# The LoRA part of a bias, summed on VectorE instead of by TensorE products

## Chip, cores and metric

The kernel runs on one core of a Trainium2 chip. The metric is device time in microseconds (us) for one execution. Before the change three runs took 56.14, 56.83 and 57.04 us, a median of 56.83 us.

## What is computed

There are 8 samples `b` of 512 tokens and 256 channels, and a condition vector of 8 gates `g` for each sample. Two residual layers follow each other:

```python
# layer 0: 8 expert matrices mixed by the gates, under a mask
w_bot = einsum('bg,got->bot', cond, weight * mask)
x = x + einsum('bnt,bot->bno', x, w_bot) + bias0
# layer 1: a base matrix and 8 gated LoRA experts of rank 16, SCALING = 2
out = einsum('btc,oc->bto', x, W_base) + b_base
h = einsum('btc,erc->bter', x, As)
x = x + out + SCALING * einsum('bter,eor,be->bto', h, Bs, cond)
```

All data are float32. The kernel merges both layers into one matrix M(b) = W1(b) W0(b) for each sample and applies it to the transposed tokens. What is left beside the matrices is one bias per sample and output channel: bias0 + b_base + W_base bias0 + SCALING * sum over (e, r) of cond[b, e] B[e, o, r] (A[e, r] . bias0). The last summand is the LoRA part of the bias. In it, 8 experts times rank 16 give 128 pairs (e, r), the number of partitions.

## The kernel before

The program is written by hand for five engines with explicit semaphores; each engine runs its list in order. P is 128 partitions, NT = 2 halves of the 256 channels, NB = 8 samples.

**Stages.** TensorE first runs 28 warm-up products and the LoRA products that make W1 of samples 0 to 3 (`lora_first`, `lora`). Then come 32 products in `mixed` (line 532), float32 with a 128-column moving side, that mix the layer-0 experts; VectorE multiplies each result by the mask into W0 (`w0`). Every matrix that enters a merge or an apply is split into a high and a low float32r part, and a `product` adds three terms: high times high (line 463), high times the second low part (line 467) and the first low part times high (line 471). From sample 2 on, TensorE's list is merge(b+1), apply(b) in turn, with `lora_pair(6)` behind apply(2).

**Who prepares what.** For a sample b in the loop:
- GpSimd (POOL) adds the identity to W0 (`eye(b)`, line 203), and makes W0_lo (`w0_lo(b)`, line 199) and W1_lo (`w1_lo(b)`, line 193). `merge(b)` waits for W1_lo(b) before its first product (line 545).
- ScalarE (ACT) makes W1_hi (`w1_hi`, 242), W0_hi (248), M_hi from PSUM (`m_hi`, 255), x_hi (262), and stores half 0 of the output with its bias (`out0`, 271). `out0(0)` waits for `bias_done` (267); behind it in ACT's list are w0_hi(4), split_x_hi(3), w1_hi(4), m_hi(3) and out0(1).
- VectorE (DVE) makes x_lo (`split_x_lo`, 360), M_lo from PSUM (`m_lo`, 367), half 1 of the output (`out1`, 375), and W1 of two samples at once from PSUM (`w1_pair`, 340). In its list behind the bias come out1(0), split_x_lo(2), m_lo(2), w1_pair(4), out1(1), split_x_lo(3), m_lo(3), out1(2), split_x_lo(4). `w1_hi(4)` waits for both halves of w1_pair(4), and `w1_lo(4)` waits for w1_hi(4).

**The bias.** ACT copies a row of bias0, which every partition holds, into PSUM (`ps_row`, line 295). VectorE takes the dot products of A's rows with it (`dot(A_er, A_bias0)`, 423; one number for each pair (e, r), on that pair's partition), scales it by the gates to `low_bias` (425, 128 x 8), and adds the two fixed biases (428). TensorE sums over the pairs behind apply(0): two float32 products of B_er with the 8 columns of low_bias (594) into the front of the bank `ps_out[3]`. VectorE waits for them (432), takes two dot products with the rows of W_base (435), and adds everything up in two instructions (439), the first from PSUM. These raise `bias_done`. apply(1) waits for it before its half 1 (560), as that half is written to the bank `ps_out[3]`.

**Loads.** All loads but two go through SyncE's queue in order: the A part of the LoRA factors, eight packs of experts and masks, x of sample 0, `rows` (W_base by rows, and bias0), then x of samples 1 to 7 (lines 148 to 157).

Of the kernel before, what the change touches and what calls it, by code (L numbers as in the profile page):

```python
# [5 lines left out]
def conditional_residual_kernel(nc: bass.Bass, head: bass.AP, rest: bass.AP, packs: bass.AP, factors_A: bass.AP,  # L6
# [7 lines left out]
    ALU = mybir.AluOpType  # L14
    ACT = mybir.ActivationFunctionType

    P = 128
    NB, _, XW = xT.shape
    NT = 2
    TOK = XW // NT  # L20
    C = base.shape[1] // NT
    H = P
    NG = 8
# [7 lines left out]
    SCALING = 32.0 / 16  # L31
# [4 lines left out]
    assert packs.shape == (NQ - 1, P, PACKW)  # L36

    OB0, OB1, OA, OBT = NB, NB + NT, NB + 2 * NT, NB + 2 * NT + C
    cut = MIXW + C

    with ExitStack() as ctx:
        def sb(name, shape, dt=f32):
            return ctx.enter_context(nc.sbuf_tensor(name, shape, dt))

        def pb(name, shape):
            return ctx.enter_context(nc.psum_tensor(name, shape, f32))

        def sem(name):
            return ctx.enter_context(nc.semaphore(name))
# [12 lines left out]
        cond_er = lora_sb[:, 0:NB]  # L62
        bias0 = lora_sb[:, OB0:OB0 + NT]
        bias1 = lora_sb[:, OB1:OB1 + NT]
        A_er = lora_sb[:, OA:OA + C]
        B_er = lora_sb[:, OBT:OBT + C]
        base_sb = sb("base_sb", [P, NT, C])
        rows_sb = sb("rows_sb", [P, NT + 1, C])
        base_rows = rows_sb[:, 0:NT, :]
        bias0_row = rows_sb[:, NT, :]  # L70
        x_sb = sb("x_sb", [P, NB, NT, TOK])

        warm = sb("warm", [P, 128], bf16)
# [1 line left out]
        ident = sb("ident", [P, P])  # L75
        row_products = sb("row_products", [P, C])
        A_bias0 = sb("A_bias0", [P, 1])
        bias_sum = sb("bias_sum", [P, NT])
        base_bias0 = sb("base_bias0", [P, NT])
        low_bias = sb("low_bias", [P, NB])  # L80
        bias_sb = sb("bias_sb", [P, NT, NB])
        A_hi = sb("A_hi", [P, C], f32r)
        A_lo = sb("A_lo", [P, C], f32r)
# [20 lines left out]
        ps_out = [pb(f"ps_out{i}", [P, TOK]) for i in range(2 * NT)]  # L104
# [5 lines left out]
        ps_last = ps_lora[0][:, 0, :]  # L110


        ps_bias = ps_out[3][:, 0:NT * NB].rearrange("p (j b) -> p j b", j=NT)
        ps_row = ps_out[3][:, C:2 * C]


# [2 lines left out]
        mix_in, lora_arrived, base_in, rows_in = sem("mix_in"), sem("lora_arrived"), sem("base_in"), sem("rows_in")  # L119
# [2 lines left out]
        x_in = [sem(f"x_in{b}") for b in range(NB)]  # L122

        warm_set, ident_zero, ident_done = sem("warm_set"), sem("ident_zero"), sem("ident_done")
        base_done, dots_done, low_done, fixed_done = sem("base_done"), sem("dots_done"), sem("low_done"), sem("fixed_done")
        row_done, bias_mm, bias_done, bhi_done, blo_done = sem("row_done"), sem("bias_mm"), sem("bias_done"), sem("bhi_done"), sem("blo_done")

        ahi_done, alo_done = sem("ahi_done"), sem("alo_done")
        lora_mm, w1_done, w1hi_done, w1lo_done = sem("lora_mm"), sem("w1_done"), sem("w1hi_done"), sem("w1lo_done")
# [16 lines left out]
        @block.sync  # L146
        def _(sp):
            sp.dma_start(lora_sb[:, 0:OBT], factors_A).then_inc(lora_arrived, 16)
            sp.dma_start(packs_sb[:, 0:cut], head).then_inc(mix_in, 16)
            sp.dma_start(packs_sb[:, cut:MIXW + PACKW], rest).then_inc(pack_in[0], 16)  # L150
            for q in range(1, NQ):
                at = MIXW + q * PACKW
                sp.dma_start(packs_sb[:, at:at + PACKW], packs[q - 1]).then_inc(pack_in[q], 16)
            for b in range(NB):
                sp.dma_start(x_sb[:, b], xT[b].rearrange("p (j n) -> p j n", j=NT)).then_inc(x_in[b], 16)
                if b == 0:
                    sp.dma_start(rows_sb[:, :, :], rows.rearrange("p (j c) -> p j c", j=NT + 1)).then_inc(rows_in, 16)

            for b in range(NB):
                for j in range(NT):  # L160
                    if b < NB - 1 or j < NT - 1:
                        sp.wait_ge(out_done[j], b + 1)
                        sp.dma_start(outT[b, j], out_sb[:, b % 2, j, :]).then_inc(stored[b % 2][j], 16)

            sp.wait_ge(last_done, 1)
            sp.dma_start(outT[NB - 1, 1, :, 0:TOK // 2],
                         out_sb[:, 1, 1, 0:TOK // 2]).then_inc(stored[1][1], 16)
            sp.wait_ge(out_done[1], NB)
            sp.dma_start(outT[NB - 1, 1, :, TOK // 2:TOK],
                         out_sb[:, 1, 1, TOK // 2:TOK]).then_inc(stored[1][1], 16)  # L170
            for i in range(2):
                for j in range(NT):
                    sp.wait_ge(stored[i][j], 16 * (NB // 2 + (i == 1 and j == 1)))
# [147 lines left out]
        def _(dve):  # L321
            nc.vector.memset(warm[:, :], 0.0).then_inc(warm_set, 1)  # L322

            def b_lo(b):
                dve.wait_ge(bhi_done, b + 1)
                nc.vector.scalar_tensor_tensor(out=B_lo[:, b], in0=B_er, scalar=cond_er[:, b:b + 1],
                                               in1=B_hi[:, b].bitcast(f32),
                                               op0=ALU.mult, op1=ALU.subtract).then_inc(blo_done, 1)
# [26 lines left out]
            def split_x_lo(b):  # L355
                dve.wait_ge(xhi_done, b + 1)

                if b >= XBUF:
                    dve.wait_ge(apply_mm, 2 * (b - XBUF + 1))
                nc.vector.tensor_tensor(x_lo[:, b % XBUF], x_sb[:, b], x_hi[:, b % XBUF].bitcast(f32),  # L360
                                        ALU.subtract).then_inc(xlo_done, 1)

            def m_lo(b):
                dve.wait_ge(mhi_done, b + 1)
                if b >= 2:
                    dve.wait_ge(apply_mm, 2 * (b - 1))
                nc.vector.tensor_tensor(M_lo[:, b % 2], ps_merge[b % 2][:, :, :], M_hi[:, b % 2].bitcast(f32),  # L367
                                        ALU.subtract).then_inc(mlo_done, 1)
# [9 lines left out]
            def dot(row, out):  # L378

                return nc.vector.tensor_tensor_reduce(out=row_products[:, :], in0=row, in1=ps_row, scale=1.0,  # L380
                                                      scalar=0.0, op0=ALU.mult, op1=ALU.add, accum_out=out)

            def ramp_low(b):
# [8 lines left out]
                                           op0=ALU.mult, op1=ALU.subtract).then_inc(alo_done, 1)  # L392
            dve.wait_ge(B_arrived, 16)
            for b in range(4):
# [20 lines left out]
            ramp_low(0)  # L415
            ramp_low(1)
            split_x_lo(0)
            b_lo(7)
            m_lo(0)

            dve.wait_ge(row_done, 1)
            dve.wait_ge(rows_in, 16)
            dot(A_er, A_bias0[:, :]).then_inc(dots_done, 1)
            dve.wait_ge(dots_done, 1)
            nc.vector.tensor_scalar(low_bias[:, :], cond_er, A_bias0[:, :], SCALING,
                                    ALU.mult, ALU.mult).then_inc(low_done, 1)

            nc.vector.tensor_tensor(bias_sum[:, :], bias0, bias1, ALU.add).then_inc(fixed_done, 1)
            m_lo(1)
            split_x_lo(1)  # L430

            dve.wait_ge(bias_mm, 1)
            for j in range(NT):
                dve.wait_ge(dots_done, 1 + j)
                dot(base_rows[:, j, :], base_bias0[:, j:j + 1]).then_inc(dots_done, 1)
            dve.wait_ge(dots_done, 1 + NT)
            dve.wait_ge(fixed_done, 1)
            for j in range(NT):
                last = nc.vector.tensor_scalar(bias_sb[:, j, :], ps_bias[:, j, :], base_bias0[:, j:j + 1],
                                               bias_sum[:, j:j + 1], ALU.add, ALU.add)  # L440
            last.then_inc(bias_done, 1)
            dve.wait_ge(bias_done, 1)
# [8 lines left out]
            b = NB - 1  # L451
# [6 lines left out]
        def _(pe):  # L458
# [92 lines left out]
            def apply(b):  # L551
                pe.wait_ge(mhi_done, b + 1)
                pe.wait_ge(xhi_done, b + 1)
                m_lo_ready = (mlo_done, b + 1)
                for i in range(NT):

                    if b >= 2:
                        pe.wait_ge(out_done[i], b - 1)
                    if b == 1 and i == 1:
                        pe.wait_ge(bias_done, 1)  # L560
                    cols = slice(i * P, (i + 1) * P)
                    whole = b < NB - 1 or i < NT - 1
                    for n in [slice(0, TOK)] if whole else [slice(0, TOK // 2), slice(TOK // 2, TOK)]:
                        bank = ps_out[b % 2 * NT + i][:, n] if n.start == 0 else ps_last
                        product(bank, [(M_hi[:, b % 2, j, cols], M_lo[:, b % 2, j, cols],
                                        x_hi[:, b % XBUF, j, n], x_lo[:, b % XBUF, j, n]) for j in range(NT)],
                                m_lo_ready if i == 0 else None,
                                (xlo_done, b + 1) if i == 0 else None).then_inc(apply_mm, 1)
# [20 lines left out]

            pe.wait_ge(w0_done, NQ)  # L590
            apply(0)
            pe.wait_ge(low_done, 1)
            for i in range(NT):
                mm = nc.tensor.matmul(ps_bias[:, i, :], B_er[:, i * P:(i + 1) * P], low_bias[:, :],  # L594
                                      start=True, stop=True)
            mm.then_inc(bias_mm, 1)
            for b in range(1, NB):
                if b + 1 < NB:
                    merge(b + 1)
# [57 lines left out]
```

## Time and profile before

| | |
|---|---|
| three runs | 56.14, 56.83, 57.04 us (median 56.83) |
| profiled execution | 56.49 us |
| its span, first to last instruction | 54.7 us |
| around the span (56.49 - 54.7) | 1.79 us |
| TensorE (PE) busy | 50.9 us, 93% of the span |
| VectorE (DVE) busy | 39.9 us, 73% |
| ScalarE (ACT) busy | 31.7 us, 58% |
| GpSimd (POOL) busy | 30.6 us, 56% |
| granted TensorE clock, mean | 1.000 |

The profile is one execution taken by the hardware profiler. Busy times of different engines overlap. A float32 product is two matmul records. An instruction's record can overlap the next one's on its engine by about a tenth of a microsecond, so the distance from start to start says what an instruction costs the engine. In the chain of waits, matmuls are laid end to end, so its start times are some tenths later than the starts in the timeline. Spans on POOL are rough.

### The profile page before, as it was taken

The page shows a single profiled execution, that of the slowest core. Times are in us where ns is not written, and L with a number is a line of the kernel's source. Part 1 is how long each engine was busy: PE and PEld are TensorE (multiplying, and loading weights), DVE is VectorE, ACT ScalarE, POOL GpSimd, SP SyncE. Part 2 cuts the span into 40 slices and gives each one's busy share as a digit, 9 for nine tenths or more (in the row PEclk, how much of TensorE's full clock was granted, in tenths as well). Part 3 has the DMA queues.
Part 4 walks back from the last instruction along what each step waited for, and adds up shares of the span by engine and source line. Part 5 has one row for each costly group of instructions (what it writes and reads, how often), then busy time and mean ns, then how long its engine had stood idle before and what let it go on. Part 6 is the DMA issues. An engine that isn't in the chain of part 4 may idle for free.

```text
span 54.7 us, 971 instructions
## 1 busy us (share of the span) xinstructions
PE 50.9 (93%) x330; PEld 46.1 (84%) x330; DVE 39.9 (73%) x64; ACT 31.7 (58%) x53; POOL 30.6 (56%) x30
## 2 busy tenths in 40 slices
PE   2999999999999999999999999999999999999900
PEld 2989999999998978998898889889889889888800
DVE  0049996989799996999999893789819949805030
ACT  1939944404935399539609961992992940840800
POOL 4004349585990099998945999999998100000000
PEclk9999999999999999999999999999999999999999
DMA  0698999999999997000820280073063064059582
GB/s 0 162 381 230 368 379 393 424 416 413 419 395 407 422 395 291 33 0 0 306 84 0 78 318 0 0 271 118 0 247 136 0 226 157 0 205 369 193 288 96
DMA packets 5476, 11.79 MB, mean 216 GB/s; under 512 B 608, under 2 KB 1376, under 8 KB 5472
## 3 DMA queue, kind: packets, MB, share of 16 engines
q1 hardware_dynamic: 5184, 11.35, 55.5%
q10 hardware_dynamic: 288, 0.39, 2.0%
q8 instruction: 2, 0.03, 0.2%
q14 instruction: 2, 0.02, 0.1%
HBM read 7.54 MB, written 4.19 MB: 215 GB/s over the span
## 4 chain that ended last, share of the span: by engine, by line
PE 93%; DVE 1%; issue 0%
PE ps_out L463 13%; PE ps_out L532 13%; PE ps_out L467 13%; PE ps_out L471 13%; PE ps_merge L463 8%; PE ps_merge L467 8%; PE ps_merge L471 8%; PE ps_merge L573 6%; PE ps_lora L477 4%; PE ps_lora L463 2%; PE ps_lora L467 2%; PE ps_lora L471 2%; DVE out_sb L454 1%; PE ps_out L594 1%; DVE warm L322 0%
## 5 line engine op out<-in xcount | busy, mean ns | idle before, releaser
L193 POOL TENSOR_TENSOR W_lo<-W,W_hi 128x512 fp32r<-128x512 f32 x8 | 12.2, 1523 | 3.8 <-ACT W_hi L242 3.7
L360 DVE TENSOR_TENSOR x_lo<-x_sb,x_hi 128x1024 fp32r<-128x1024 f32 x8 | 11.7, 1466 | 0.0
L463 PE MATMUL ps_out<-x_hi,M_hi 128*128 128x512 f32 (+1 forms) x32 | 9.8, 388 | 0.0
L255 ACT ACTIVATE M_hi<-ps_merge 128x512 fp32r<-128x512 f32 x8 | 4.8, 595 | 8.5 <-PE ps_merge L471 8.5
L467 PE MATMUL ps_out<-x_lo,M_hi 128*128 128x512 f32 (+1 forms) x32 | 9.7, 384 | 0.0
L471 PE MATMUL ps_out<-x_hi,M_lo 128*128 128x512 f32 (+1 forms) x32 | 9.7, 383 | 0.0
L199 POOL TENSOR_TENSOR W_lo<-W,W_hi 128x512 fp32r<-128x512 f32 x6 | 9.4, 1574 | 0.4 <-ACT W_hi L248 0.3
L262 ACT ACTIVATE x_hi<-x_sb 128x1024 fp32r<-128x1024 f32 x8 | 8.5, 1057 | 0.0
L375 DVE TENSOR_SCALAR out_sb<-ps_out,bias_sb 128x512 f32<-128x512 f32 x7 | 5.2, 748 | 4.0 <-PE ps_out L471 3.9
L532 PE MATMUL ps_out<-packs_sb 128*128 128x128 f32 x64 | 7.3, 275 | 0.0
L532 PEld LDWEIGHTS ps_out<-packs_sb 128*128 128x128 f32 x64 | 7.2, 192 | 0.0
L242 ACT ACTIVATE W_hi<-W 128x512 fp32r<-128x512 f32 x8 | 5.0, 629 | 3.8 <-DVE W L332 1.9
L203 POOL TENSOR_TENSOR W<-W,ident 128x256 f32<-128x256 f32 x6 | 5.5, 929 | 2.8 <-DVE x_lo L360 2.8
L467 PEld LDWEIGHTS ps_out<-x_lo,M_hi 128*128 128x128 f32 x32 | 5.9, 188 | 1.2
L471 PEld LDWEIGHTS ps_out<-x_hi,M_lo 128*128 128x128 f32 x32 | 5.9, 188 | 1.2
L367 DVE TENSOR_TENSOR M_lo<-ps_merge,M_hi 128x512 fp32r<-128x512 f32 x8 | 5.5, 686 | 1.9 <-ACT M_hi L255 1.9
L271 ACT ACTIVATE out_sb<-ps_out,bias_sb 128x512 f32<-128x512 f32 x8 | 5.5, 684 | 2.2 <-PE ps_out L471 2.2
L463 PE MATMUL ps_merge<-W_hi 128*128 128x256 f32 x32 | 6.6, 287 | 0.0
L467 PE MATMUL ps_merge<-W_lo,W_hi 128*128 128x256 f32 x32 | 6.4, 283 | 0.0
L471 PE MATMUL ps_merge<-W_hi,W_lo 128*128 128x256 f32 x32 | 6.4, 283 | 0.0
L463 PEld LDWEIGHTS ps_out<-x_hi,M_hi 128*128 128x128 f32 x32 | 5.5, 189 | 0.9 <-issue 0.2
L349 DVE TENSOR_TENSOR W<-ps_out,packs_sb 128x512 f32<-128x512 f32 x8 | 5.3, 686 | 1.1 <-PE ps_out L532 1.1
(65 smaller groups left out, 73.7 us busy)
## 6 DMA issues: line engine op xcount, KB each, us to landing
x_sb<-xT_dram SPq DMA_DIRECT2D x8, 512.0 KB, 10.8
outT_dram<-out_sb SPq DMA_DIRECT2D x15, 256.0 KB, 2.3
packs_sb<-packs_dram SPq DMA_DIRECT2D x7, 288.0 KB, 5.6
rows_sb<-rows_dram SPq DMA_DIRECT2D x1, 384.0 KB, 7.3
base_sb<-base_dram ACTq DMA_DIRECT2D x1, 256.0 KB, 3.5
outT_dram<-out_sb SPq DMA_DIRECT2D x2, 128.0 KB, 1.8
packs_sb<-head_dram SPq DMA_DIRECT2D x1, 192.0 KB, 3.3
packs_sb<-rest_dram SPq DMA_DIRECT2D x1, 160.0 KB, 4.6
```

The lines of the kernel that those rows point to most:

```text
L193: pool.tensor_tensor(W1_lo[:, b % W1BUF], W1[:, b % W1BUF], W1_hi[:, b % W1BUF].bitcast(f32), ALU.subtract).then_inc(w1lo_done, 1)
L199: pool.tensor_tensor(W0_lo[:, b % 2], W0[:, b], W0_hi[:, b % 2].bitcast(f32), ALU.subtract).then_inc(w0lo_done, 1)
L203: pool.tensor_tensor(diagonal(b), diagonal(b), ident[:, :].unsqueeze(1).to_broadcast([P, NT, P]), ALU.add).then_inc(eye_done, 1)
L262: nc.scalar.activation(x_hi[:, b % XBUF], x_sb[:, b], ACT.Copy).then_inc(xhi_done, 1)
L271: nc.scalar.activation(out_sb[:, b % 2, 0, :], ps_out[b % 2 * NT][:, :], ACT.Identity, bias=bias_sb[:, 0, b:b + 1]).then_inc(out_done[0], 1)
L349: nc.vector.tensor_tensor(W0[:, :, :, ts].rearrange("p b j t -> p j b t"), ps_mix[q % 4][:, :].rearrange("p (j b t) -> p j b t", j=NT, t=T ...
L360: nc.vector.tensor_tensor(x_lo[:, b % XBUF], x_sb[:, b], x_hi[:, b % XBUF].bitcast(f32), ALU.subtract).then_inc(xlo_done, 1)
L367: nc.vector.tensor_tensor(M_lo[:, b % 2], ps_merge[b % 2][:, :, :], M_hi[:, b % 2].bitcast(f32), ALU.subtract).then_inc(mlo_done, 1)
L463: nc.tensor.matmul(out, hi_l, hi_r, start=(n == 0), stop=False)
L467: nc.tensor.matmul(out, hi_l, lo_r, start=False, stop=False)
L471: mm = nc.tensor.matmul(out, lo_l, hi_r, start=False, stop=(n == len(terms) - 1))
L532: mm = nc.tensor.matmul(dst[:, j, :, k, :], pack(q)[0][:, k, j * P:(j + 1) * P], mix, start=True, stop=True)
```

## The change

VectorE sums the LoRA part of the bias itself. For this, `rows` also brings B by rows (for each output channel its 128 pairs) and all 64 gates, on every partition: 1088 instead of 768 floats per partition. TensorE turns the column `A_bias0` to a row that every partition holds, by one float32 product: the column, repeated 128 times, is the stationary side and the identity the moving side. VectorE then multiplies this row by B's rows and by SCALING (`B_products`, 128 x 256), sums over the rank (`expert_bias`, 128 x 16), multiplies by the gates (`cond_products`, 128 x 128) and sums over the gates (`low_bias`, now 128 x 16 with output channels on the partitions). Each of the four waits for the one before. `dot(A_er, ...)` moves ahead of m_lo(0), b_lo(7) behind m_lo(0). The gate of apply(1)'s half 1 now asks for the dot products and `B_products` rather than the finished bias.

```diff
-        rows_sb = sb("rows_sb", [P, NT + 1, C])
+        rows_sb = sb("rows_sb", [P, ROWS])
...
-        ps_bias = ps_out[3][:, 0:NT * NB].rearrange("p (j b) -> p j b", j=NT)
+        A_bias0_row = ps_out[3][:, 0:P]
...
-            b_lo(7)
-            m_lo(0)
-
             dve.wait_ge(row_done, 1)
             dve.wait_ge(rows_in, 16)
             dot(A_er, A_bias0[:, :]).then_inc(dots_done, 1)
-            dve.wait_ge(dots_done, 1)
-            nc.vector.tensor_scalar(low_bias[:, :], cond_er, A_bias0[:, :], SCALING,
-                                    ALU.mult, ALU.mult).then_inc(low_done, 1)
-
+            m_lo(0)
+            b_lo(7)
             nc.vector.tensor_tensor(bias_sum[:, :], bias0, bias1, ALU.add).then_inc(fixed_done, 1)
             m_lo(1)
             split_x_lo(1)
 
-            dve.wait_ge(bias_mm, 1)
+            dve.wait_ge(turned, 1)
             for j in range(NT):
                 dve.wait_ge(dots_done, 1 + j)
                 dot(base_rows[:, j, :], base_bias0[:, j:j + 1]).then_inc(dots_done, 1)
+
+            dve.wait_ge(turned, 1)
+            nc.vector.scalar_tensor_tensor(out=B_products[:, :, :], in0=A_bias0_row.unsqueeze(1).to_broadcast([P, NT, P]),
+                                           scalar=SCALING, in1=B_rows, op0=ALU.mult, op1=ALU.mult).then_inc(sums_done, 1)
+            dve.wait_ge(sums_done, 1)
+            nc.vector.tensor_reduce(expert_bias[:, :, :], B_products[:, :, :].rearrange("p j (g r) -> p j g r", g=NG),
+                                    mybir.AxisListType.X, ALU.add).then_inc(sums_done, 1)
+            dve.wait_ge(sums_done, 2)
+            nc.vector.tensor_tensor(cond_products[:, :, :, :], expert_bias[:, :, :].unsqueeze(2).to_broadcast([P, NT, NB, NG]),
+                                    cond_row.unsqueeze(1).to_broadcast([P, NT, NB, NG]), ALU.mult).then_inc(sums_done, 1)
+            dve.wait_ge(sums_done, 3)
+            nc.vector.tensor_reduce(low_bias[:, :, :], cond_products[:, :, :, :],
+                                    mybir.AxisListType.X, ALU.add).then_inc(sums_done, 1)
             dve.wait_ge(dots_done, 1 + NT)
             dve.wait_ge(fixed_done, 1)
+            dve.wait_ge(sums_done, 4)
             for j in range(NT):
-                last = nc.vector.tensor_scalar(bias_sb[:, j, :], ps_bias[:, j, :], base_bias0[:, j:j + 1],
+                last = nc.vector.tensor_scalar(bias_sb[:, j, :], low_bias[:, j, :], base_bias0[:, j:j + 1],
                                                bias_sum[:, j:j + 1], ALU.add, ALU.add)
...
                     if b == 1 and i == 1:
-                        pe.wait_ge(bias_done, 1)
+
+                        pe.wait_ge(dots_done, 1 + NT)
+                        pe.wait_ge(sums_done, 1)
...
-            pe.wait_ge(low_done, 1)
-            for i in range(NT):
-                mm = nc.tensor.matmul(ps_bias[:, i, :], B_er[:, i * P:(i + 1) * P], low_bias[:, :],
-                                      start=True, stop=True)
-            mm.then_inc(bias_mm, 1)
+
+            pe.wait_ge(dots_done, 1)
+            pe.wait_ge(ident_done, 1)
+            nc.tensor.matmul(A_bias0_row, A_bias0[:, :].to_broadcast([P, P]), ident[:, :],
+                             start=True, stop=True).then_inc(turned, 1)
```

## Rows read from the trace of the kernel before

**Rows 1.** The profile's page: busy time by engine, and one load.
```profile
PE 50.9 (93%) x330; PEld 46.1 (84%) x330; DVE 39.9 (73%) x64; ACT 31.7 (58%) x53; POOL 30.6 (56%) x30
...
rows_sb<-rows_dram SPq DMA_DIRECT2D x1, 384.0 KB, 7.3
```

**Rows 2.** The chain of waits: start us, us, what.
```profile
7.90 7.14 PE ps_out L532 x64
...
19.31 0.70 PE ps_out L463 x2
...
20.46 0.45 PE ps_out L471 x2
...
22.27 0.34 PE ps_out L594 x4
22.62 0.34 PE ps_merge L463 x2
...
28.34 0.47 PE ps_out L463 x2
...
32.45 0.23 PE ps_merge L463 x2
...
40.81 0.23 PE ps_merge L463 x2
```

**Rows 3.** Timeline of POOL: start us, us, instruction, idle time before it.
```profile
23.70 1.29 POOL L199 TENSOR_TENSOR W_lo<-W,W_hi 128x512 fp32r<-128x512 f32 x1
24.95 0.75 POOL L203 TENSOR_TENSOR W<-W,ident 128x256 f32<-128x256 f32 x1
...
29.32 2.20 POOL L193 TENSOR_TENSOR W_lo<-W,W_hi 128x512 fp32r<-128x512 f32 x1 [1.39 <-ACT W_hi L242]
...
37.63 2.27 POOL L193 TENSOR_TENSOR W_lo<-W,W_hi 128x512 fp32r<-128x512 f32 x1
```

**Rows 4.** Timeline of ACT.
```profile
15.86 0.39 ACT L295 ACTIVATE ps_out<-rows_sb 128x256 f32<-128x256 f32 x1 [0.72 <-DVE W L349]
...
18.61 0.60 ACT L255 ACTIVATE M_hi<-ps_merge 128x512 fp32r<-128x512 f32 x1 [1.29 <-PE ps_merge L471]
...
28.61 0.63 ACT L242 ACTIVATE W_hi<-W 128x512 fp32r<-128x512 f32 x1 [1.77 <-DVE W L340]
```

**Rows 5.** Timeline of DVE.
```profile
18.86 0.48 DVE L326 SCALAR_TENSOR_TENSOR B_lo<-lora_sb,B_hi 128x256 fp32r<-128x256 f32 x1
19.25 0.68 DVE L367 TENSOR_TENSOR M_lo<-ps_merge,M_hi 128x512 fp32r<-128x512 f32 x1
...
20.31 0.37 DVE L425 TENSOR_SCALAR low_bias<-lora_sb,A_bias 128x8 f32<-128x8 f32 x1
20.59 0.15 DVE L428 TENSOR_TENSOR bias_sum<-lora_sb 128x2 f32<-128x2 f32 x1
...
21.80 1.34 DVE L360 TENSOR_TENSOR x_lo<-x_sb,x_hi 128x1024 fp32r<-128x1024 f32 x1
...
23.51 0.42 DVE L380 CUSTOM_DVE_ANT_0 row_products<-rows_sb,ps_out 128x256 f32<-128x256 f32 x1
23.86 0.08 DVE L380 DVE_READ_ACCUMULATOR2_ANT base_bias<- 128x1 f32 x1
23.98 0.48 DVE L439 TENSOR_SCALAR bias_sb<-ps_out,base_bias,bias_sum 128x8 f32<-128x8 f32 x2
...
25.16 1.62 DVE L360 TENSOR_TENSOR x_lo<-x_sb,x_hi 128x1024 fp32r<-128x1024 f32 x1
26.71 0.68 DVE L367 TENSOR_TENSOR M_lo<-ps_merge,M_hi 128x512 fp32r<-128x512 f32 x1
27.31 1.27 DVE L340 TENSOR_TENSOR W<-ps_lora,base_sb 128x512 f32<-128x512 f32 x2
...
29.16 1.21 DVE L360 TENSOR_TENSOR x_lo<-x_sb,x_hi 128x1024 fp32r<-128x1024 f32 x1
```

**Rows 6.** Timeline of SyncE's queue.
```profile
6.38 0.65 SPq L157 DMA_DIRECT2D rows_sb<-rows_dram  x1
```

More of the change, by code:

```diff
@@ L38, in conditional_residual_kernel @@
     OB0, OB1, OA, OBT = NB, NB + NT, NB + 2 * NT, NB + 2 * NT + C
+    OBR = (NT + 1) * C
+    OCR = OBR + NT * P
+    ROWS = OCR + NB * NG
     cut = MIXW + C
@@ L67, in conditional_residual_kernel @@
         base_sb = sb("base_sb", [P, NT, C])
-        rows_sb = sb("rows_sb", [P, NT + 1, C])
-        base_rows = rows_sb[:, 0:NT, :]
-        bias0_row = rows_sb[:, NT, :]
+        rows_sb = sb("rows_sb", [P, ROWS])
+        base_rows = rows_sb[:, 0:NT * C].rearrange("p (j c) -> p j c", j=NT)
+        bias0_row = rows_sb[:, NT * C:OBR]
+        B_rows = rows_sb[:, OBR:OCR].rearrange("p (j r) -> p j r", j=NT)
+        cond_row = rows_sb[:, OCR:ROWS].rearrange("p (b g) -> p b g", b=NB)
         x_sb = sb("x_sb", [P, NB, NT, TOK])
@@ L79, in conditional_residual_kernel @@
         base_bias0 = sb("base_bias0", [P, NT])
-        low_bias = sb("low_bias", [P, NB])
+        B_products = sb("B_products", [P, NT, P])
+        expert_bias = sb("expert_bias", [P, NT, NG])
+        cond_products = sb("cond_products", [P, NT, NB, NG])
+        low_bias = sb("low_bias", [P, NT, NB])
         bias_sb = sb("bias_sb", [P, NT, NB])
@@ L124, in conditional_residual_kernel @@
         warm_set, ident_zero, ident_done = sem("warm_set"), sem("ident_zero"), sem("ident_done")
-        base_done, dots_done, low_done, fixed_done = sem("base_done"), sem("dots_done"), sem("low_done"), sem("fixed_done")
-        row_done, bias_mm, bias_done, bhi_done, blo_done = sem("row_done"), sem("bias_mm"), sem("bias_done"), sem("bhi_done"), sem("blo_done")
+        base_done, dots_done, sums_done, fixed_done = sem("base_done"), sem("dots_done"), sem("sums_done"), sem("fixed_done")
+        row_done, turned, bias_done, bhi_done, blo_done = sem("row_done"), sem("turned"), sem("bias_done"), sem("bhi_done"), sem("blo_done")
         ahi_done, alo_done = sem("ahi_done"), sem("alo_done")
@@ L156, in _ @@
                 if b == 0:
-                    sp.dma_start(rows_sb[:, :, :], rows.rearrange("p (j c) -> p j c", j=NT + 1)).then_inc(rows_in, 16)
+                    sp.dma_start(rows_sb[:, :], rows).then_inc(rows_in, 16)
             for b in range(NB):
@@ L638 @@
                            A_er, Bs.transpose(0, 2, 1).reshape(G * R, C)], axis=1)
-    rows = np.concatenate([halves(base), np.broadcast_to(bias0, (P, C))], axis=1)
+    rows = np.concatenate([halves(base), np.broadcast_to(bias0, (P, C)), halves(Bs.transpose(1, 0, 2)),
+                           np.broadcast_to(cond.reshape(-1), (P, NB * G))], axis=1)
     xT = np.ascontiguousarray(x.transpose(0, 2, 1).reshape(NB, NT, P, TOK).transpose(0, 2, 1, 3).reshape(NB, P, NT * TOK))
```

## The prediction

> **What bounds the kernel now.** I read the page first. TensorE is busy 50.9 of 54.7 us, DVE 39.9, POOL 30.6 [rows 1]. The chain of waits then runs through TensorE alone from the warm-up to the last product; the bias products (line 594) are a link of it, so what TensorE saves there counts if nobody else becomes late. Next I read the timelines of POOL, ACT and DVE, to see how early each delivers what TensorE waits for. The tight place is merge(4), which asks for W1_lo(4). That lies at the end of a path: bias_done, out1(0), x_lo(2), m_lo(2), w1_pair(4) on DVE, w1_hi(4) on ACT, w1_lo(4) on POOL. ACT sat idle 1.77 us until w1_pair(4), POOL 1.39 us until w1_hi(4) [rows 3, 4]: every step there is tied to DVE. W1_lo(4) is complete at 29.32 + 2.20 = 31.52, and merge(4)'s link starts at 32.45 [rows 2, 3].
>
> How much of this gap is slack, I take from the one place where TensorE did wait in this part. M_hi(0) was complete at 18.61 + 0.60 = 19.21 [rows 4], and the first pair of apply(0) ended at 19.31 + 0.70 = 20.01 in the chain, where such a pair otherwise takes 0.47 [rows 2]. From release to the effective start it is 20.01 - 0.47 - 19.21 = 0.33 us. So merge(4) needs its release at 32.45 - 0.33 = 32.12, and the slack is **0.60 us**. Further on, W1_lo(6) ends at 37.63 + 2.27 = 39.90, merge(6) starts at 40.81: slack 0.58, the same [rows 2, 3]. POOL works without a pause from 29.32 until then, so what it loses at w1_lo(4) stays lost up to merge(6). The last merge has much more room.
>
> **TensorE's own part.** Removed: the four records of line 594, 0.34 us, and most likely the lengthening behind them, as the next pair takes 0.34 where 0.23 is usual: 0.11. Added: one float32 product with 128 columns, two records at 7.14/64 = 0.112, so 0.22 [rows 2]. Net 0.34 + 0.11 - 0.22 = **0.23 us saved**. The stationary side with a step of zero has no row; I take it as a load like any other, and between nothing and twice the product's price the saving lies between 0 and 0.45.
>
> **DVE ahead of the turn.** dot(A) now stands ahead of m_lo(0), and takes some 0.45 (0.35 to the accumulator read, 0.08, a gap) where b_lo(7) took 0.39 start to start [rows 5]. M_lo(0) comes 0.06 later, at 19.99; the products that use it start in the chain at 20.46, less 0.33 is 20.13 [rows 2, 5]. Covered by 0.14, cost nothing; without that cover 0.06. Behind m_lo(0) b_lo(7) is needed only by lora_pair(6) ten microseconds later, and the removed low_bias instruction (0.28 start to start) had idle time behind it: m_lo(1) waits for ACT. The turn is done where the bias products were, so the base dot products start at 23.06 as now.
>
> **DVE's sum, the term that decides.** The accumulator read ends at 23.94 [rows 5]. Then:
> - B_products, 256 elements a partition: 0.48 as B_lo; the dot product over 256 elements took 0.42. 23.95 to 24.43.
> - First reduction, no row: from below 0.30, the dot's work with less fixed time; from above 0.60. I take 0.42, the dot over as many elements. With 0.04 to see the semaphore (23.94 to 23.98), it ends at 24.89.
> - Gates times experts, 128 elements: between 0.15 (2 elements) and 0.42 (256 elements), in the middle 0.28 [rows 5].
> - Second reduction, 128 elements: likewise 0.28.
> - The two last additions 0.48, as now.
>
> Undisturbed: 0.48 + 0.42 + 0.28 + 0.28 and four gaps of 0.04 = 1.62 us. bias_done moves from 24.46 to about 26.1; all values at their lower ends (0.42, 0.30, 0.15, 0.15) give 1.2, at their upper ends (0.48, 0.60, 0.42, 0.42) 2.1.
>
> The page "VectorE: DVE Perf Modes" of the Trainium skill puts such instructions lower; its section on the TRN2 errata gives 58 cycles plus the elements from SBUF and 120 plus the elements from PSUM, at 0.96 GHz. By that page the four would be 0.39, 0.33, 0.19 and 0.19, an estimate of 1.10 + 0.16 = 1.26 in all. This case's row disagrees: by that page the additions (8 elements from PSUM) would take 0.13 each, and the trace has 0.48 for two [rows 5].
>
> **Contention on top.** DVE and POOL hold each other up when both read two tensors in SBUF: x_lo takes 1.21 alone, and 1.62 when it starts at 25.16 under POOL's eye(5), which ends at 25.70; w1_lo(4) takes 2.20 where w0_lo(3) takes 1.29, because x_lo(3) began 0.16 before it [rows 3, 5]. The gates' product reads two SBUF tensors. It is ready at 24.93, while w0_lo(3) ends at 24.99 and eye(5) starts at 24.95. If DVE comes first, it loses about 0.05. The additions now read SBUF; the old low_bias instruction did, during a POOL instruction, and took 0.37. As eye(5) would then run until some 26.0 and the additions start at 25.6, I add 0.25. Sum: 1.62 + 0.05 + 0.25 = **1.92 us** later bias_done.
>
> **What of it reaches the end.** out1(0) and out0(0) start 1.92 later; both only delay their own engines, the output has a buffer. x_lo(2) comes at 27.1, when eye(5) is over, so it costs 1.21 and not 1.62: 0.41 comes back. m_lo(2) then ends at 27.39 + 1.51 = 28.90; its products start two pairs behind 28.34, at 28.34 + 2 x 0.47 = 29.28, less 0.33 and less 0.23 saved is 28.72, so TensorE waits 0.18 there, ahead of the larger wait and not added to it [rows 2, 5]. w1_pair(4), w1_hi(4) and w1_lo(4) are 1.51 late, the last again behind x_lo(3), which moves with it: W1_lo(4) at 33.03. TensorE's merge(4) is then at 33.36 in place of 32.45: 1.51 - 0.60 = **0.91 us late**. TensorE's saving of 0.23 is swallowed, since it only arrives earlier at the wait. merge(5) and merge(6) stay late by the same amount, and all behind them with it. The rule to use: end = delay of bias_done - 0.41 - 0.60, but not below -0.23.
>
> **The gate of apply(1).** It opens with B_products at 24.43, against bias_done at 24.46 now: nothing changes. **The load**: `rows` grows by 160 KB, from 384 KB. It was issued at 6.4 and took 7.3 us, landing at 13.7; were it longer in proportion to its size (by 7.3 x 160/384 = 3.0 us), it would land at 16.7, 0.8 after ACT's copy started at 15.86 [rows 1, 4, 6]. But its time is mostly queueing behind packs already issued, so I take a few tenths, under 2.1 us of cover, and nothing for the later x loads.
>
> **The rivals.**
> 1. *POOL gets in first* (chance 0.27). If eye(5) (0.75 us from 24.95) beats the gates' product, that waits until about 25.57, by the x_lo of 25.16. Then 25.57 + 0.28, the reduction 0.32, the additions 0.52 give 26.7: 2.2 late, with slower reductions 2.6. End: +1.2 to +1.6, or 57.9 to 58.3 us, slower by over 2%. It speaks for it that the two are 0.02 apart; against it, x_lo at 21.80 got in between two POOL instructions. The page "SBUF — State Buffer" of the Trainium skill, section "Who interferes with whom", has this as a rule: whoever issues first holds the shared ports for the whole instruction, a product of two SBUF tensors contends with POOL's reads, a reduction never. The trace agrees for the products (2.20 against 1.29); for the reduction no row shows it.
> 2. *Cheap small instructions* (0.12). With the sum at 1.3 and little contention, the end is 1.35 - 1.01 = +0.3, some 57.0 us.
> 3. *Not slower: the order at w1_lo(4) flips* (0.11). If x_lo(3) starts over 0.16 us later relative to w1_hi(4) than now, POOL goes first and w1_lo(4) takes 1.3 instead of 2.2. That gives back 0.9: 0.91 - 0.9 = 0.0, some 56.7 us; flipped with a shorter sum, it ends down to 0.2 below before. Against it: both follow from w1_pair(4) by fixed steps, so the 0.16 should stay.
> 4. *The load is late* (0.02), landing at 16.7: ACT's list stops for 0.8 at line 295, ahead of W0_hi of half 1, and merge(0) with it: up to +0.8, or 57.5.
>
> **The numbers.** My forecast has 0.48. The profiled execution took 56.49 us, 0.34 below the median of 56.83; by it the sum is 57.40, by the median 57.74. I take **57.6**, near the middle. Forecast alone: delay 1.6 to 2.1, so 57.1 to 58.0. The range reaches to rival 1's upper half and rival 3: 56.4 to 58.5. What a measurement can tell from no change is about 2%, 1.14 us. Slower by more takes rival 1 and a little of the forecast's top, 0.31; faster by more would need over 1 us where TensorE gives 0.23: 0.03 for what I don't see; the rest, 0.66, lies within.
>
> **What would show it.** In the profile after: bias additions ending near 26.4; POOL's first L193 behind x 29.3 starting near 30.8; TensorE with an idle gap ahead of merge(4) named after POOL's W_lo; PE's busy time lower by a few tenths and the span longer. If DVE's four instructions come to under 1 us, there is no gap and the end is 0.2 earlier: the forecast is then wrong. It is wrong too if the gap is there and closes again before merge(6).

## The result and the profile after

Over 22 runs of each, the kernel before took 56.60 us (median; 56.04 to 57.29) and the changed kernel 57.18 us (56.66 to 57.83). The ratio is 1.0103, with a 95% interval of 1.0069 to 1.0138: **slower by 0.58 us, or 1.0%**. The medians are over all runs; the ratio leaves out the slower runs of each kernel, over 1.5% above its fastest. The forecast was 0.91 us of loss and 57.6 us, with a range of 56.4 to 58.5.

The page after, first its engines. TensorE is busy half a microsecond less than in [rows 1] (part of it at the start, as the last section tells), and yet the span is 55.0 us in place of 54.7:

```profile
PE 50.4 (92%) x328; PEld 45.2 (82%) x328; DVE 40.7 (74%) x67; ACT 31.9 (58%) x53; POOL 31.1 (57%) x30
```

The chain of waits after (start us, us, what). It answers to [rows 2]:

```profile
7.56 7.14 PE ps_out L551 x64
...
21.94 0.22 PE ps_out L616 x2
22.16 0.24 PE ps_merge L482 x2
...
31.92 0.59 issue
32.51 0.48 PE ps_merge L482 x2
32.99 0.23 PE ps_merge L486 x2
...
36.92 0.25 PE ps_merge L482 x2
...
41.12 0.25 PE ps_merge L482 x2
...
52.31 0.48 DVE out_sb L473
```

The last piece of the same view before:

```profile
51.99 0.48 DVE out_sb L454
```

Two profiled executions differ at the start, up to the expert products (7.90 us before, 7.56 after; the last section tells why). So I count from the start of those products: 51.99 - 7.90 = **44.09** us before, 52.31 - 7.56 = **44.75** after, a loss of 0.66. The new product is one link of 0.22, and the pair behind it takes 0.24, not 0.34: TensorE is 0.22 ahead there. Then a gap of 0.59 opens ahead of merge(4), and its first pair is lengthened too (0.48 for the usual 0.23). merge(5) and merge(6) follow without a gap of their own.

DVE after, answering to [rows 5]:

```profile
18.52 0.41 DVE L389 CUSTOM_DVE_ANT_0 row_products<-lora_sb,ps_out 128x256 f32<-128x256 f32 x1
...
18.91 0.69 DVE L376 TENSOR_TENSOR M_lo<-ps_merge,M_hi 128x512 fp32r<-128x512 f32 x1
19.52 0.95 DVE L335 SCALAR_TENSOR_TENSOR B_lo<-lora_sb,B_hi 128x256 fp32r<-128x256 f32 x1
...
23.53 0.08 DVE L389 DVE_READ_ACCUMULATOR2_ANT base_bias<- 128x1 f32 x1
23.53 0.42 DVE L443 SCALAR_TENSOR_TENSOR B_products<-ps_out,rows_sb 128x256 f32<-128x256 f32 x1
23.98 0.42 DVE L446 TENSOR_REDUCE expert_bias<-B_products 128x16 f32<-128x256 f32 x1
24.44 0.37 DVE L449 TENSOR_TENSOR cond_products<-expert_bias,rows_sb 128x128 f32<-128x128 f32 x1
24.85 0.29 DVE L452 TENSOR_REDUCE low_bias<-cond_products 128x16 f32<-128x128 f32 x1
25.27 0.48 DVE L458 TENSOR_SCALAR bias_sb<-low_bias,base_bias,bias_sum 128x8 f32<-128x8 f32 x2
...
26.46 1.22 DVE L369 TENSOR_TENSOR x_lo<-x_sb,x_hi 128x1024 fp32r<-128x1024 f32 x1
27.59 0.68 DVE L376 TENSOR_TENSOR M_lo<-ps_merge,M_hi 128x512 fp32r<-128x512 f32 x1
28.19 1.28 DVE L349 TENSOR_TENSOR W<-ps_lora,base_sb 128x512 f32<-128x512 f32 x2
...
30.04 1.22 DVE L369 TENSOR_TENSOR x_lo<-x_sb,x_hi 128x1024 fp32r<-128x1024 f32 x1
```

POOL after, answering to [rows 3], and the weight load that waited:

```profile
24.63 0.78 POOL L212 TENSOR_TENSOR W<-W,ident 128x256 f32<-128x256 f32 x1
...
30.21 2.19 POOL L202 TENSOR_TENSOR W_lo<-W,W_hi 128x512 fp32r<-128x512 f32 x1 [1.37 <-ACT W_hi L251]
```

```profile
32.48 0.30 PEld L482 LDWEIGHTS ps_merge<-W_hi 128*128 128x128 f32 x2 [0.99 <-ACT W_hi L257]
```

W1_lo(4) is complete at 30.21 + 2.19 = 32.40, the weight load starts at 32.48. The trace names ACT's W_hi as the releaser, but that had long ended (27.06); the last of merge(4)'s waits to be met is POOL's.

### The profile page after: what moved, and what is told of

Its sections match the earlier page's. It is cut to its first block, busy times and chain, and to the rows that moved or that the text cites. A ratio compares the mean times of both kernels' runs of the same rounds, so it can differ in the third digit from the quotient of the medians.

```text
span 55.0 us, 972 instructions
## 1 busy us (share of the span) xinstructions
PE 50.4 (92%) x328; PEld 45.2 (82%) x328; DVE 40.7 (74%) x67; ACT 31.9 (58%) x53; POOL 31.1 (57%) x30
## 4 chain that ended last, share of the span: by engine, by line
PE 86%; DMA 5%; issue 2%; ACT 1%; DVE 1%
PE ps_out L482 13%; PE ps_out L551 13%; PE ps_out L486 13%; PE ps_out L490 13%; PE ps_merge L482 8%; PE ps_merge L490 8%; PE ps_merge L486 8%; DMA lora_sb<-factors_B_dram 5%; PE ps_lora L496 3%; PE ps_lora L490 2%; PE ps_lora L486 2%; PE ps_lora L482 2%; ACT B_hi L243 1%; DVE out_sb L473 1%; PE ps_out L616 0%
## 5 line engine op out<-in xcount | busy, mean ns | idle before, releaser
L202 POOL TENSOR_TENSOR W_lo<-W,W_hi 128x512 fp32r<-128x512 f32 x8 | 13.2, 1644 | 3.2 <-ACT W_hi L251 3.0
L369 DVE TENSOR_TENSOR x_lo<-x_sb,x_hi 128x1024 fp32r<-128x1024 f32 x8 | 11.0, 1376 | 0.2 <-ACT x_hi L271 0.2
L208 POOL TENSOR_TENSOR W_lo<-W,W_hi 128x512 fp32r<-128x512 f32 x6 | 9.2, 1526 | 2.0 <-ACT W_hi L257 2.0
L482 PEld LDWEIGHTS ps_merge<-W_hi 128*128 128x128 f32 x32 | 5.1, 190 | 1.6 <-ACT W_hi L257 1.0
```

Of the source, the lines that this page charges most:

```text
L202: pool.tensor_tensor(W1_lo[:, b % W1BUF], W1[:, b % W1BUF], W1_hi[:, b % W1BUF].bitcast(f32), ALU.subtract).then_inc(w1lo_done, 1)
L208: pool.tensor_tensor(W0_lo[:, b % 2], W0[:, b], W0_hi[:, b % 2].bitcast(f32), ALU.subtract).then_inc(w0lo_done, 1)
L482: nc.tensor.matmul(out, hi_l, hi_r, start=(n == 0), stop=False)
```

## The experiments

Each kernel was timed beside the kernel before. The table has the ratio to it with its 95% interval, and from one profile of each two distances from the start of the expert products, as change against before (16.56 and 44.09 us): when bias_done is raised, and the end. e9 and e11 are the same kernel, and their ends differ by 0.02. "Rule" is the forecast's rule, end = delay of bias_done - 0.41 - 0.60, at least -0.23.

| kernel | ratio | interval | bias_done | end | rule |
|---|---|---|---|---|---|
| changed | 1.0103 | 1.0069 to 1.0138 | +1.63 | +0.66 | +0.62 |
| e1 load only | 0.9969 | 0.9928 to 1.0010 | -0.01 | +0.03 | 0.0 |
| e2 no sums | 0.9997 | 0.9947 to 1.0047 | +1.25 | +0.31 | +0.24 |
| e3 sums added to before | 1.0096 | 1.0047 to 1.0146 | +1.71 | +0.75 | +0.70 |
| e4 out1(0) on ACT | 0.9975 | 0.9915 to 1.0036 | +1.63 | +0.01 | -0.04 |
| e6 order flipped | 1.0201 | 1.0142 to 1.0260 | +1.63 | +0.75 | - |
| e7 no sums, PSUM source | 0.9932 | 0.9887 to 0.9978 | -0.01 | -0.20 | -0.23 |
| e8 sums twice | 1.0335 | 1.0262 to 1.0408 | +2.70 | +1.72 | +1.69 |
| e9 e4 and split W1 | 0.9909 | 0.9858 to 0.9961 | +1.63 | -0.19 | -0.23 |
| e10 e9's edits on before | 1.0001 | 0.9960 to 1.0043 | 0.00 | +0.01 | 0.0 |
| e11 e9 again | 0.9962 | 0.9908 to 1.0015 | +1.63 | -0.21 | -0.23 |

For e4 the rule has 0.66 more to take off, as out1(0) is gone from DVE; for e9 and e11 that and the split of w1_pair(4), which brings it to its lower bound. e2 and e7 leave the LoRA part out of the bias and serve only to measure.

**e1, the load alone.** The kernel before with

```diff
-                    sp.dma_start(rows_sb[:, :, :], rows.rearrange("p (j c) -> p j c", j=NT + 1)).then_inc(rows_in, 16)
+                    sp.dma_start(rows_sb[:, :], rows).then_inc(rows_in, 16)   # 1088 floats, not 768
```

> The kernel before with the larger `rows` load (1088 floats per partition in place of 768), its new part unused. Path theory (the time is lost on the way bias_done - out1(0) - w1_pair(4) - w1_hi(4) - w1_lo(4) - merge(4)): +0.0 us against before, within 0.1, since the load is needed only at ACT's line 295. Load theory (the longer transfer is what costs): +0.5 us or more, the whole measured loss of 0.58, and a wait for a DMA on ACT.

Measured 0.9969 and +0.03: the larger load costs nothing. On e1's page it takes 7.5 us from issue to landing, where the smaller one took 7.3. The load theory falls.

**e2, the sums left out.**

```diff
-            nc.vector.scalar_tensor_tensor(out=B_products[:, :, :], ...
-            nc.vector.tensor_reduce(expert_bias[:, :, :], ...
-            nc.vector.tensor_tensor(cond_products[:, :, :, :], ...
-            nc.vector.tensor_reduce(low_bias[:, :, :], ...
-                last = nc.vector.tensor_scalar(bias_sb[:, j, :], low_bias[:, j, :], ...
+                last = nc.vector.tensor_scalar(bias_sb[:, j, :], B_rows[:, j, 0:NB], ...
```

> The changed kernel without its four sum instructions on DVE (the additions read rows of B in place of the LoRA part, which is left out of the bias). Path theory: bias_done comes about when it did before, there is no gap ahead of merge(4), and TensorE's saving of 0.23 us shows: -0.2 us against before, 0.8 below the changed kernel. Load theory: +0.5 us, as the load is still the larger one. If the turn by TensorE cost more than two records of 0.11 us, the end is above -0.1.

A miss: by the profile +0.31, not -0.2. The timed ratio, 0.9997 with 0.5% to each side (-0.30 to +0.27 us), does not decide it: it takes in -0.2 and ends just under +0.31. DVE's timeline of e2, then POOL's:

```profile
24.44 1.73 DVE L446 TENSOR_SCALAR bias_sb<-rows_sb,base_bias,bias_sum 128x8 f32<-128x8 f32 x2
26.21 0.75 DVE L384 TENSOR_SCALAR out_sb<-ps_out,bias_sb 128x512 f32<-128x512 f32 x1
```

```profile
24.16 1.29 POOL L208 TENSOR_TENSOR W_lo<-W,W_hi 128x512 fp32r<-128x512 f32 x1
25.41 0.73 POOL L212 TENSOR_TENSOR W<-W,ident 128x256 f32<-128x256 f32 x1
```

The two additions of 8 columns, now from SBUF, took 1.73 us: the first lasted 1.04 us, until POOL's W0_lo(3) had ended (25.45), the second 0.78, until eye(5) had (they ended at 26.17 and 26.14). In the changed kernel the four sums delay the additions until eye(5) is nearly over (25.41), and they take 0.48. So e2 removed one cost and met another in its place; e7 takes both away.

**e7, sums left out and the additions from PSUM.**

```diff
-                last = nc.vector.tensor_scalar(bias_sb[:, j, :], low_bias[:, j, :], ...
+                last = nc.vector.tensor_scalar(bias_sb[:, j, :], A_bias0_row[:, j * NB:(j + 1) * NB], ...
...
+                        pe.wait_ge(bias_done, 1)   # apply(1)'s gate, as in the kernel before
```

> The changed kernel without its four sum instructions (the LoRA part is left out of the bias), and the two additions read the turned row in PSUM, as they read PSUM before, in place of SBUF. Contention theory (in e2 the additions took 1.73 us for 0.48, because they read SBUF while POOL worked from 24.2 to 26.1): they take 0.48 again, there is no gap ahead of merge(4), and the end is at -0.2 us against before. If the additions' SBUF source is not the cause, they stay long and the end is at +0.2 to +0.3 as in e2's profile.

The same line in e7:

```profile
23.66 0.48 DVE L446 TENSOR_SCALAR bias_sb<-ps_out,base_bias,bias_sum 128x8 f32<-128x8 f32 x2
```

0.48 again, bias_done at its old distance, no gap, and the end at -0.20: this is TensorE's saving, seen by itself (0.9932, interval under 1). The SBUF source beside a working POOL was the cause in e2: e8, below, has the additions from SBUF with POOL idle, and they take 0.48.

**e3, the sums added to the kernel before.** TensorE's products stay, `rows` is the larger one, and apply(1)'s gate asks for the additions and B_products; behind the old additions stand

```diff
+            nc.vector.scalar_tensor_tensor(out=B_products[:, :, :], in0=ps_row[:, 0:P].unsqueeze(1).to_broadcast([P, NT, P]), ...
...
+            nc.vector.tensor_reduce(low_sums[:, :, :], cond_products[:, :, :, :],
+                                    mybir.AxisListType.X, ALU.add).then_inc(bias_done, 1)
```

> The kernel before with TensorE's two bias products kept, and the four sum instructions put behind the additions as extra work (their result is unused; they read a row of bias0 from PSUM in place of the turned one); bias_done is raised by the last of them, and apply(1)'s gate asks for the additions and B_products only. Path theory: the delay of bias_done is again about 1.6 us, 0.4 comes back at x_lo(2), 0.6 is slack, so +0.6 us against before, the same as the changed kernel, since TensorE's 0.23 is swallowed by the wait there. Additive theory (the saving and the loss add up at the end): +0.8 us, 0.23 above the changed kernel.

Measured 1.0096, close to the changed kernel's ratio. By the profile the end is +0.75, but its bias_done is also 0.08 later than the changed kernel's; the rule gives +0.70, the additive theory +0.93. The 0.22 us that TensorE saves do not show once it has to wait.

e3 also shows the order that rival 1 of the prediction feared. POOL's eye(5) got in ahead of the product with the gates; POOL's line, then DVE's:

```profile
24.49 0.74 POOL L213 TENSOR_TENSOR W<-W,ident 128x256 f32<-128x256 f32 x1
```

```profile
24.82 0.56 DVE L458 TENSOR_TENSOR cond_products<-expert_bias,rows_sb 128x128 f32<-128x128 f32 x1
```

The product took 0.56 and ended behind eye(5), at 25.38 and 25.23.

**e8, the sums twice.**

```diff
+            nc.vector.tensor_reduce(expert_bias[:, :, :], B_products[:, :, :].rearrange("p j (g r) -> p j g r", g=NG), ...
+            nc.vector.tensor_tensor(cond_products[:, :, :, :], ...
+            nc.vector.tensor_reduce(low_bias[:, :, :], ...
```

> The changed kernel with the reduction, the product with the gates and the second reduction done twice: 1.1 to 1.2 us more on DVE ahead of bias_done. Path theory: the end goes up one for one, as all slack is used: +1.7 us against before (1.6 to 1.9). x_lo(2) and M_lo(2) are now late for apply(2) too and make a gap of about 1 us there, which is not added but taken off the one ahead of merge(4). If such gaps add up: +2.5 us or more.

Measured 1.0335, or 1.9 us of 56.77, and by the profile +1.72. bias_done moved by 1.07 beyond the changed kernel, the end by 1.06: one for one. The earlier waits, at apply(2), do not add up. e8's chain of waits there and at merge(4):

```profile
30.52 0.61 PE ps_out L499 x2
...
33.90 0.67 issue
34.57 0.47 PE ps_merge L491 x2
```

Counted from the expert products, the third pair of apply(2) is in effect 0.75 us later than before (30.52 + 0.61 - 0.46 - 8.55 = 22.12 against 29.27 - 7.90 = 21.37); behind merge(4)'s wait it is 1.71 (34.57 + 0.47 - 0.23 - 8.55 = 26.26 against 32.45 - 7.90 = 24.55), about the end's 1.72. The second wait takes in the first.

In DVE's timeline of e8, POOL's eye(5) runs from 25.59 to 26.37, and POOL is idle from then until 29.20:

```profile
25.81 0.28 DVE L452 TENSOR_REDUCE low_bias<-cond_products 128x16 f32<-128x128 f32 x1
26.13 0.42 DVE L455 TENSOR_REDUCE expert_bias<-B_products 128x16 f32<-128x256 f32 x1
26.58 0.29 DVE L458 TENSOR_TENSOR cond_products<-expert_bias,rows_sb 128x128 f32<-128x128 f32 x1
26.91 0.29 DVE L461 TENSOR_REDUCE low_bias<-cond_products 128x16 f32<-128x128 f32 x1
27.33 0.48 DVE L467 TENSOR_SCALAR bias_sb<-low_bias,base_bias,bias_sum 128x8 f32<-128x8 f32 x2
```

The product takes 0.29 with POOL idle and 0.37 beside it. The second reduction takes 0.28 beside POOL and 0.29 with it idle. The gap ahead of the additions is 0.13 (27.20 to 27.33) with POOL idle, as long as in the changed kernel.

**e4, out1(0) on ACT.** The changed kernel with

```diff
                 nc.scalar.activation(out_sb[:, b % 2, 0, :], ps_out[b % 2 * NT][:, :], ACT.Identity,
                                      bias=bias_sb[:, 0, b:b + 1]).then_inc(out_done[0], 1)
+                if b == 0:
+                    act.wait_ge(apply_mm, 2)
+                    nc.scalar.activation(out_sb[:, 0, 1, :], ps_out[1][:, :], ACT.Identity,
+                                         bias=bias_sb[:, 1, 0:1]).then_inc(out1_first, 1)
...
-                out1(b - 1)
+                if b > 1:
+                    out1(b - 1)
```

The semaphores of SyncE and TensorE that counted out1(0) are changed with it.

> The changed kernel with out1(0) taken from DVE's list and done by ACT right behind out0(0), where ACT is idle 1.5 us before w1_hi(4). Path theory: x_lo(2) and w1_pair(4) come 0.66 us earlier, W1_lo(4) too, and the gap ahead of merge(4) shrinks from 0.6 to under 0.1 us: the end is at 0.0 us against before (between -0.1 and +0.1), 0.6 below the changed kernel. Theory that DVE's load as a whole, or the new product on TensorE, costs the time: +0.4 us or more.

Measured 0.9975 and +0.01. bias_done is as late as in the changed kernel, and the loss is gone: it was on the way from bias_done to W1_lo(4), and not in the new product. TensorE's saving does not show yet, as merge(4)'s first pair still takes 0.43 for 0.23. DVE's load is 40.0 us here, back near the 39.9 of before, so e4 does not separate the path from the load; e11 below does, with 40.7 us of load, as in the changed kernel, and no loss.

**e6, the order at w1_lo(4) flipped.**

```diff
-                    split_x_lo(b + 1)
-                    m_lo(b + 1)
+                    if b == 2:
+                        m_lo(b + 1)
+                        split_x_lo(b + 1)
+                    else: ...
```

> The changed kernel with x_lo(3) and m_lo(3) in the other order on DVE, so that w1_lo(4) on POOL starts ahead of x_lo(3). Rival 3 of the prediction: w1_lo(4) takes 1.3 us in place of 2.2, the 0.9 us come back, and the end is at 0.0 to -0.2 us against before. Saturated theory (POOL has no pause from w1_lo(4) to w1_lo(6), and x_lo(3) holds it up at whatever instruction it meets): the gap ahead of merge(4) goes, but one of about the same length comes ahead of merge(5), and the end stays at +0.6 us.

POOL's timeline of e6, then e6's chain of waits:

```profile
31.00 1.30 POOL L202 TENSOR_TENSOR W_lo<-W,W_hi 128x512 fp32r<-128x512 f32 x1 [1.38 <-ACT W_hi L251]
32.25 1.73 POOL L212 TENSOR_TENSOR W<-W,ident 128x256 f32<-128x256 f32 x1
```

```profile
36.89 0.68 issue
37.57 0.48 PE ps_merge L486 x2
```

w1_lo(4) takes 1.30 and merge(4) has no gap, but eye(6) behind it now takes 1.73 for 0.7, and a gap of 0.68 stands ahead of merge(5). The saturated theory holds and rival 3 of the prediction falls, in its price: the flip gives nothing back. The timed ratio of 1.0201 is higher than the profile's +0.75 us (1.3%); what makes the rest was not settled.

**e9, a version that keeps the gain.** e4, and W1(4) ahead of W1(5); `w1_hi(4)` waits for W1(4) alone:

```diff
-                act.wait_ge(w1_done, b + 1 if b < SINGLE else b // 2 * 2 + 2)
+                act.wait_ge(w1_done, b + 1 if b < SINGLE + 2 else b // 2 * 2 + 2)
...
+                if b == SINGLE:
+                    for s in range(2):
+                        for j in range(NT):
+                            add = nc.vector.tensor_tensor(W1[:, at + s, j, :], ps_lora[j][:, s, :], base_sb[:, j, :], ALU.add)
+                        add.then_inc(w1_done, 1)
+                    return
```

> The changed kernel with out1(0) on ACT as in e4, and w1_pair(4) split by sample, so that W1(4) is complete after two instructions of 256 columns (about 0.7 us) in place of 1.2, and w1_hi(4) starts about 0.5 us earlier than in e4. Path theory: no gap ahead of merge(4), and TensorE's 0.23 us shows at last: -0.2 us against before, 56.4 us. If POOL's unbroken run up to merge(5) and merge(6) sets the end instead (w1_lo(4) now starts ahead of x_lo(3)): a gap of 0.1 to 0.3 us ahead of merge(5), and 0.0 to +0.1.

Its chain of waits has no gap at any merge:

```profile
7.98 7.14 PE ps_out L565 x64
...
51.88 0.48 DVE out_sb L487
```

51.88 - 7.98 = 43.90, 0.19 under before.

**e10 and e11, whose gain it is.** e10 puts the two edits of e9 on the kernel before; e11 is e9 again.

> The kernel before with the same two edits as e9 (out1(0) on ACT, w1_pair(4) split by sample). Path theory: merge(4) has its slack of 0.60 us there already, and TensorE's list is unchanged, so 0.0 us against before (between -0.1 and +0.1). If the two edits help by themselves, -0.2 us or more, and e9 owes its gain to them and not to the changed bias.

> The kernel of e9 once more, beside e10 on the same chip. Path theory: -0.2 us against before and 0.2 below e10; from the start of the expert products to the end of the kernel 43.9 us against 44.1.

e10 is at 1.0001 and +0.01: the edits alone give nothing. e11 has -0.21 by its profile, though DVE is busy 40.7 us and bias_done 1.63 late, both as in the changed kernel: neither costs anything once the way behind is short enough. The timed ratios of e9 and e11 are 0.9909 and 0.9962; the second's interval takes in 1, so the 0.2 us (0.4%) are shown by the profiles and only in part by the times.

## Why the prediction was right

- **The place** was right: the gap ahead of merge(4), set by W1_lo(4). e4 and e9 remove it by shortening the way, e8 lengthens it one for one.
- **TensorE's 0.23** was right (0.22 in the chain, 0.20 in e7), and so was that it is swallowed (e3). The stationary side with a step of zero, which had no row, came at the product's usual price: a link of 0.22.
- **The slack of 0.60** was right: W1_lo(4) came 1.22 later from the start of the expert products (32.40 - 7.56 against 31.52 - 7.90), merge(4) 0.65 later. From release to effective start it took 32.99 - 0.23 - 32.40 = 0.36 where I had 0.33.
- **The 0.41 given back** at x_lo(2) was right: 1.22 in place of 1.62, and 1.63 of delay became 1.22. M_lo(0), forecast 0.06 later, was not later at all (18.91 - 7.56 against 19.25 - 7.90). b_lo(7) took 0.95 where it stands now, twice its 0.48, but m_lo(1) behind it still had to wait for ACT.
- **The delay of bias_done** was mis-sized: 1.92 forecast, 1.63 measured. This is the term that failed, in size alone; its 0.29 cover the 0.25 between the forecast's 0.91 and the profile's 0.66. B_products was given 0.49 from the end of the accumulator read, and took 0.34 (23.61 to 23.95): it started with the read, not behind it. Contention was given 0.30, and 0.08 of it is shown, on the gates' product (0.37 against 0.29); the additions took 0.48 as before. Against these stands a term that the sum did not have: the gap ahead of the additions is 0.13 and not 0.04, in e8 too, where POOL is idle. Its cause was not tested. The two reductions, which had no row, came at 0.42 and 0.29 for the forecast 0.42 and 0.28.
- **The wait at apply(2)**, forecast at 0.18, did not come: the chain has no gap there. M_lo(2) was complete at 28.27 - 7.56 = 20.71, 0.29 ahead of the forecast's 28.90 - 7.90 = 21.00, which is the same mis-sized term.
- **The time itself**, 57.6 against 57.18, is 0.33 off by the loss (0.91 against 0.58). The rest, about 0.1, is the time of the kernel before: the forecast set out from some 56.7, between the profiled execution and the median of three runs, and the median over 22 runs is 56.60.
- **Rival 1** did not happen: the gates' product started at 24.44, ahead of eye(5) at 24.63. The forecast had the two 0.02 apart; they came 0.19 apart, mostly as the product was ready 0.15 sooner (24.44 - 7.56 against 24.93 - 7.90). What it lost, 0.08, it lost beside W0_lo(3), which ran until 24.66. The order that rival 1 feared did occur in e3, where it cost the product 0.27 (0.56 against 0.29). The rule of the Trainium skill that it leaned on (SBUF — State Buffer, "Who interferes with whom") is borne out by the rows: a product of two SBUF tensors was held up by a POOL instruction that had started first (e3), and a reduction was not (0.28 beside POOL, 0.29 with it idle, in e8).
- **Rival 2** fell: the reductions took 0.42 and 0.29. The estimate for them from the Trainium skill (VectorE: DVE Perf Modes, the section on the TRN2 errata) was 0.33 and 0.19, too low by 0.09 and 0.10; the trace decides.
- **Rival 3** did not happen: x_lo(3) began 0.17 ahead of w1_lo(4) (30.04 and 30.21), for 0.16 before, and w1_lo(4) took 2.19. e6 shows besides that the flip would have given nothing back.
- **Rival 4 and the load**: covered, as e1 shows; in the changed kernel too the load took 7.3 us, as before.

## What to carry to other kernels

Work taken off the engine that bounds the kernel pays only if the work put in its place stays within the slack of those who feed it. Read that slack from the trace, from the deliverer's end to the waiting link's start less the restart, and follow the moved work through every list behind it up to the next such wait. Here POOL ran without a pause downstream, and swapping the order of two instructions that hold each other up only moved the gap to the next deadline (e6); a shorter path ahead of it is what helped (e4, e9).

## What the runs showed of the hardware

Small instructions from SBUF can wait once for each instruction of POOL: two additions of 8 columns took 1.04 and 0.78 us beside two POOL instructions, 1.73 together (e2). They took 0.48 from PSUM (e7), and 0.48 from SBUF with POOL idle (e8).

The start of the expert products varies by up to 1.1 us between the profiles (7.43 us in e3, 8.55 in e8), more than the effect studied. The twelve LoRA products ahead of the expert products took 1.76 us in the changed kernel's profile and 2.87 in e1's. TensorE's timeline of the changed kernel, then of e1:

```profile
5.12 0.28 PE L496 MATMUL ps_lora<-B_hi,A_hi 128*128 128x256 f32 x1
5.23 0.28 PE L496 MATMUL ps_lora<-B_hi,A_lo 128*128 128x256 f32 x1
```

```profile
5.11 0.41 PE L482 MATMUL ps_lora<-B_lo,A_hi 128*128 128x256 f32 x1
5.33 0.41 PE L482 MATMUL ps_lora<-B_hi,A_hi 128*128 128x256 f32 x1
```

Products of 256 columns start 0.11 to 0.12 us apart in one and 0.21 to 0.22 in the other. That is about 2.4 and 1.2 columns per ns, the paces of TensorE's two clock levels, though the profile's granted clock reads 1.00 in this stretch of both. The kernel before changes from the one pace to the other within the twelve (2.24 us). What sets the moment of the change was not tested. Up to the expert products TensorE's list is the same in all kernels here. This is why the ends above are counted from the start of the expert products.
